# Value matmuls of four attention heads together, in two column parts, inside a transformer kernel on one core

## The reference, cut to what matters

```
scores = jnp.einsum('bhqd,bhkd->bhqk', q, k) * hs ** (-0.5)
p = jax.nn.softplus(scores)
p = p * p
causal = jnp.tril(jnp.ones((t, t), dtype=p.dtype))
p = p * causal
attn = p / (jnp.sum(p, axis=-1, keepdims=True) + 1e-09)
out = jnp.einsum('bhqk,bhkd->bhqd', attn, v)
```

## Time and profile before

| | us |
|---|---|
| median of three runs | 1726.71 |
| the profiled execution, its own time | 1729.62 |
| span of its profile | 1727.8 |
| attention phase, first score matmul to last divide | about 275.6 to 748.9 |

### The profile page before, as it was taken

The page is one execution under the profiler, slowest core; times in us unless marked ns, Lnnn a source line. Parts: engine busy times, 40 slices in busy tenths (PEclk is TensorE's granted clock), DMA queues, the critical chain, the costliest instruction groups (busy, mean ns, idle before and its releaser), DMA issues. The chain is left out here.

```text
span 1727.8 us, 28806 instructions
## 1 busy us (share of the span) xinstructions
PE 1643.6 (95%) x11141; PEld 1148.6 (66%) x11188; DVE 1244.1 (72%) x2350; ACT 878.2 (51%) x1356; POOL 412.0 (24%) x382
## 2 busy tenths in 40 slices
PE   8999888999999999999999999998999999899998
PEld 7888775333333433378887777776777777677786
DVE  4545897677777777656556888876877777788886
ACT  3332687666666666643232322218888887622210
POOL 0002112121212111140004422211455555311111
PEclk9999999999999999999999999999999999999999
DMA  5000266646363554200001000001322333200000
GB/s 158 14 1 13 74 195 133 88 52 96 50 90 59 79 69 73 27 1 13 1 1 41 27 1 1 1 1 64 99 99 99 99 100 115 82 13 13 25 25 25
DMA packets 57160, 95.82 MB, mean 55 GB/s; under 512 B 7904, under 2 KB 29632, under 8 KB 57024
## 3 DMA queue, kind: packets, MB, share of 16 engines
q1 hardware_dynamic: 56064, 93.38, 24.4%
q10 hardware_dynamic: 960, 0.59, 0.1%
HBM read 76.91 MB, written 17.04 MB: 54 GB/s over the span
## 5 line engine op out<-in xcount | busy, mean ns | idle before, releaser
L1405 ACT ACTIVATE att_weights<-ps 128x1024 f32<-128x1024 f32 (+1 forms) x288 | 280.7, 976 | 157.1 <-PE ps L1346 83.0
L1432 DVE TENSOR_TENSOR att_weights<-att_weights 128x1024 f32<-128x1024 f32 (+1 forms) x240 | 298.5, 1262 | 67.8 <-ACT att_weights L1405 67.1
L1366 PE MATMUL ps<-att_weights,att_v_ones 64*32 64x64 f32 (+5 forms) x2048 | 286.8, 398 | 6.2 <-DVE v L1453 6.2
L928 DVE SCALAR_TENSOR_TENSOR X<-ps,moe_gsel,X 128x256 f32<-128x256 f32 x512 | 246.1, 483 | 63.5 <-PE ps L48 40.4
L48 PE MATMUL ps<-w_experts_hi,moe_xh 128*128 128x512 f32 x512 | 204.9, 400 | 0.6 <-DVE X L928 0.6
L48 PE MATMUL ps<-w_experts_hi,moe_xl 128*128 128x512 f32 x512 | 203.1, 397 | 0.0
L48 PE MATMUL ps<-w_experts_lo,moe_xh 128*128 128x512 f32 x512 | 201.4, 393 | 0.0
L1366 PEld LDWEIGHTS ps<-att_weights,att_v_ones 128*32 128x32 f32 (+1 forms) x2048 | 81.8, 108 | 124.7 <-issue 74.1
L424 ACT ACTIVATE ffn_gates<-ps,ffn_gate_bias 128x512 f32<-128x512 f32 x72 | 49.5, 688 | 148.3 <-PE ps L48 126.6
L1495 POOL TENSOR_TENSOR att_weights<-att_weights 128x1024 f32<-128x1024 f32 x16 | 30.3, 1892 | 378.0 <-ACT att_weights L1405 378.0
L48 PEld LDWEIGHTS ps<-w_experts_hi,moe_xh 128*128 128x128 f32 x512 | 96.1, 188 | 27.4 <-DVE X L928 4.0
(11 more groups left out here) (281 smaller groups left out, 3726.8 us busy)
## 6 DMA issues: line engine op xcount, KB each, us to landing
ssm_lb<-decays SPq DMA_DIRECT2D x32, 512.0 KB, 4.6
ssm_rise<-decays SPq DMA_DIRECT2D x28, 512.0 KB, 3.9
qk_parts<-qkv_part SPq DMA_DIRECT2D x32, 384.0 KB, 2.8
q_stack<-qk_parts SPq DMA_DIRECT2D x64, 128.0 KB, 4.6
k_stack<-qk_parts SPq DMA_DIRECT2D x64, 128.0 KB, 7.9
att_q_stack<-qk_parts SPq DMA_DIRECT2D x64, 128.0 KB, 4.6
att_k_stack<-qk_parts SPq DMA_DIRECT2D x64, 128.0 KB, 8.4
out<-X SPq DMA_DIRECT2D x7, 512.0 KB, 3.2
```

What stands on the lines that cost most here:

```text
L928: dve.scalar_tensor_tensor(out=x, in0=ring[:, e // 2, (e % 2) * C:(e % 2 + 1) * C], scalar=gsel[:, s, j, e:e + 1], in1=x, op0=ALU.mult, op ...
L1366: ins = pe.matmul(O(qb)[h * 2 * HD:(h + 1) * 2 * HD, q0:q0 + w], values, Wt[rows, u % WU, t, c:c + w], start=kj == 0 and part == FULL, sto ...
L1405: act.activation(Wt[:, u % WU, 0:n], scores(u)[:, 0:n], ACT.Softplus).then_inc(p_done, 1)
L1432: dve.tensor_tensor(wt, wt, wt, ALU.mult).then_inc(sq_done["dve"], 1)
```

## The change

The values of a step's four heads are now computed together, in the order of the steps and not of the units. A step's matmuls are cut into two parts by columns, and one part is issued behind each of the two score units that are issued with the step: a FULL step into columns 0 to 255 and 256 to 511 of all four heads, a REST step into its first and second key tile. The FULL step of the first key tile, whose matmuls start the sums, is not cut: all of it is the second part. UPPER steps have one part, as before. A step's part 0 waits for the squares of both its units.

Scores run four steps ahead (`STEPS_AHEAD`), in place of seven units. The turn of a block comes two units behind its end in place of four. ScalarE squares units 6, 9 and 14 in place of 8 and 14; VectorE has 14 of a pass's 18 units in place of 15.

```diff
-    AHEAD = 7
-    TURN_LAG, COPY_LAG, DEN_LAG, OUT_LAG = 4, 7, 9, 10
+    step_units = [[u for u in range(NU) if step_of[u] == m] for m in range(NS)]
+    STEPS_AHEAD = 4
+    TURN_LAG, COPY_LAG, DEN_LAG, OUT_LAG = 2, 7, 9, 10
...
-    BY_ACT, BY_POOL = (8, 14), (11,)
+    BY_ACT, BY_POOL = (6, 9, 14), (11,)
...
-            def value_unit(i, u):
-                m = step_of[u]
+            def value_part(i, m, part_no, parts):
                 s, (qb, last, products) = m // PS, pass_steps[m % PS]
+                upper = products[0][-1] == UPPER
+                if part_no == 0:
+                    value_waits(i, m, s, qb, products, upper)
+                if products[0][-1] == FULL and parts == 2 and products[0][1] == 0:
+                    products = products if part_no else []
+                elif products[0][-1] == FULL and parts == 2:
+                    at = part_no * (BANK // 2)
+                    products = [(h, kj, unit, t, c + at, q + at, BANK // 2, part) for h, kj, unit, t, c, q, w, part in products]
+                elif parts == 2:
+                    at = part_no * len(products) // 2
+                    products = products[at:at + len(products) // 2]
+                for h, kj, unit, t, c, q, w, part in products:
+                    q0 = q - qb * BANK
...
+                    ins = pe.matmul(O(qb)[h * 2 * HD:(h + 1) * 2 * HD, q0:q0 + w], values,
+                                    Wt[rows, (s * PU + unit) % WU, t, c:c + w], start=kj == 0 and part == FULL, stop=part == UPPER and kj == (qb + 1) * GT - 1)
+                if part_no == parts - 1:
+                    ins.then_inc(pv_done, 1)
+
+            def value_waits(i, m, s, qb, products, upper):
+                if m % PS == 0:
                     pe.wait_ge(v_copied, 2 * (2 * i + s + 1))
-                if products[0][1:3] == (0, u % PU) and products[0][-1] != UPPER:
+                if products[0][1] == 0 and not upper:
                     pe.wait_ge(o_done, (i * 2 + s) * BLOCKS + qb + 1)
                     if qb == 0:
                         pe.matmul(O(qb), ident16[:, :], neg[:, 0:1].broadcast_to([P, BANK]), start=True, stop=False)
-                pe.wait_ge(sq_done[squarer[u]], squares(squarer[u], i, u))
-                if products[0][-1] == UPPER:
+                for u in step_units[m]:
+                    pe.wait_ge(sq_done[squarer[u]], squares(squarer[u], i, u))
+                if upper:
                     pe.sem_inc(squared, 1)
...
             def body(i, first=False, last=False):
-                for u in range(NU):
-                    if not (last and u + AHEAD >= NU):
-                        score_unit(i, u + AHEAD)
-                    value_unit(i, u)
-                    outputs_at(u, BLOCK_UNITS, NU, TURN_LAG, i, first, turn_output)
+                for m in range(NS):
+                    ahead = m + STEPS_AHEAD
+                    coming = [] if last and ahead >= NS else step_units[ahead % NS]
+                    parts = len(step_units[m])
+                    for n in range(2):
+                        if n < len(coming):
+                            score_unit(i + ahead // NS, coming[n])
+                        if n < parts:
+                            value_part(i, m, n, parts)
+                    for u in step_units[m]:
+                        outputs_at(u, BLOCK_UNITS, NU, TURN_LAG, i, first, turn_output)
...
-            for u in range(AHEAD):
-                score_unit(0, u)
+            for m in range(STEPS_AHEAD):
+                for u in step_units[m]:
+                    score_unit(0, u)
```

More of the change, by code:

```diff
@@ L1347, in score_unit @@
                 ins.then_inc(s_done, 1)
-            def value_unit(i, u):
-                m = step_of[u]
+            def value_part(i, m, part_no, parts):
                 s, (qb, last, products) = m // PS, pass_steps[m % PS]
-                if u % PU == 0:
+                upper = products[0][-1] == UPPER
[11 more added lines that the diff above has]
+                    q0 = q - qb * BANK
+                    rows = slice(h % 2 * HALF, (h % 2 + 1) * HALF) if part == UPPER else slice(0, P)
+                    values = va_up[rows, s, kj, h // 2] if part == UPPER and h % 2 else va[rows, s, kj, h]
+                    ins = pe.matmul(O(qb)[h * 2 * HD:(h + 1) * 2 * HD, q0:q0 + w], values,
[4 more added lines that the diff above has]
+                if m % PS == 0:
                     pe.wait_ge(v_copied, 2 * (2 * i + s + 1))
-                if products[0][1:3] == (0, u % PU) and products[0][-1] != UPPER:
+                if products[0][1] == 0 and not upper:
                     pe.wait_ge(o_done, (i * 2 + s) * BLOCKS + qb + 1)
```

## The result

The changed kernel takes **1615.35 us** (median of 4 runs, 1613.91 to 1618.04) against 1726.64 for the kernel before beside it: ratio 0.9354, 95% interval 0.9335 to 0.9373. 1613 was forecast. The profiled execution took 1616.52 us.

What follows compares the result with a forecast made beforehand. TensorE was taken to set each pass: 29.57 us becomes 21.58 plus 0.63 waiting for ScalarE, 22.2. Over 16 passes, with less saved in the last, 1726.7 - 114 = 1613 us, range 1602 to 1641.

Steps and rivals of the forecast that it cites:

- Full speed for four: TensorE's value matmuls: four heads side by side take 0.45 us a part, so eight steps fall from 14.24 to 7.20.
- rival B: Value matmuls: four wide is not full speed while other engines work; at 0.8, a pass of 24.0, 1641 us; chance 0.07.
- Rival C: Value matmuls: heads still start in pairs whatever their order; a pass of 28.6, 1711 us; chance 0.02.
- Switches and the output wait: TensorE: 0.10 us gaps between scores and values fall from 3.60 to 3.00 a pass; the 0.41 wait for divided output goes.
- ScalarE's stretch: Softpluses and squares from softplus 6 to 11 run without idle time; TensorE waits 0.6 us before unit 14's scores.
- The turn's cover: At the earlier turn, VectorE's copy is there at 2.0 and TensorE arrives at 2.4: covered by 0.4 us only.
- rival A: Hand-overs between engines: late turn 0.5 us, output wait stays, ScalarE's stretch costs double; a pass of 24.2, 1644 us; chance 0.21.
- VectorE: Its work in a pass falls from 21.2 to 20.1 us with one square less, under the 22.2 of the pass.
- rival D: TensorE's clock falls in new waits: slower, 1897 us with all of the phase at the low level; chance 0.03.
- Loads. Covered.: A pass's 2.1 MB of q and k stacks load in 15 to 17 us; the shorter pass leaves 22.
- The likeliest case: The forecast's own case for the attention passes: from no wait, 21.58 a pass (1602), to 22.8 (1621); chance 0.67.

Runs made afterwards that it cites:

- pairs: The changed kernel with a step's two parts again two pairs of heads over all columns, in place of four heads together: 1686.23 us (one run).
- one-block kernel: The changed kernel with a step's values in one block behind its second score unit: 1608.08 us; also with ScalarE squaring 8, 14 and an earlier copy: 1600.85 us.
- (8, 14): The changed kernel with ScalarE squaring units 8 and 14 in place of 6, 9 and 14: 1622.64 us, ratio 0.9394.
- paced: Each stack load piece waits for more score units: changed kernel 1613.41 us; one-block kernel with ScalarE squaring 8, 14 and an earlier copy 1593.4 us.

## Why the prediction was right

**Full speed for four (rival B).** Right: a part of 256 columns 0.57 with its switch against 0.55 of the sum, and at pairs the pass is 4.66 longer. By rival B's 0.8 the pass would have been 24.0; it is 22.29. Rival C's 28.6 fell by the same rows.

**Switches and the output wait.** Right: 0.10 at each switch that was read, and no wait for the divide in the list of waits. The one-block kernel bears the price out: with 10 blocks in place of 15 it has ten switches fewer, 1.0 us at 0.10. Its pass is 0.81 shorter although the reported wait for ScalarE is 0.41 longer, which makes 1.2; the other 0.2 I can't assign.

**ScalarE's stretch.** Right to 0.07 us at each of its eight steps: with the start of unit 7's scores at 484.28 as time 0, softplus 8 was forecast at 487.27 and starts at 487.25, softplus 11 at 490.98 and starts at 490.91. TensorE's wait is 0.60 against 0.63. The other squares of the experiments move that wait, to 0.25 with (8, 14).

**The turn's cover.** Right, 0.46 against 0.4, but the text didn't say what it hangs on. One square ahead of the copy uses it up, 0.67 a pass; that is rival A's late turn, one wait of its three, and it came only where unit 6's square went back to VectorE.

**VectorE.** 19.4 us in 22 makes 19.7 a pass against 20.1; 21.2 in 22 still don't set the pass. The clock (rival D) stayed at 1.00 from 305 us on.

**What the sum missed.** A pass is 22.29 and not 22.21, and the first one 22.77, where the wait before unit 14's scores is reported as 1.22 us, not 0.43. "Loads. Covered." asked only whether the loads end in time; they do, but TensorE stood twice amid them, as inferred above for its instructions, and that cost 3.2 us. Together the phase saved 109.2 us in place of 114.7. The whole came nearer, 111.3 by the medians, and that is partly luck: in the profiled executions 3.9 us of the difference came from outside the phase, where nothing was changed. The likeliest case's range, 1602 to 1621, held the time.

## What to carry to other kernels

When a stage has one engine at its limit, add up that engine's matmuls and gaps until the sum meets the measured period; a change is then priced by its terms. Walk the next engine through the stage unit by unit, since its average (here 18.6 us in 22.2) hides the stretch where it is late. Where a wait sits on a small instruction in an in-order queue, look at what stands ahead of it there before moving work to another engine: the copy one place earlier gave more than a third square on ScalarE.

## What the runs showed that I had not expected

TensorE can stand 0.6 to 2.7 us with no semaphore to blame while loads for a later pass are queued on the DMA engines. It did so in every unpaced kernel with four heads together that loads its stacks; the kernel before and the one with pairs issue the same loads at once too, in longer passes (29.57 and 26.95), and have none: no wait over 0.41 between 300 and 725 us, and none at all between 300 and 680. The same bytes in the same time kept the DMA engines busy for 0.71 (the changed kernel) and 0.69 (one block) of 300 to 600 us when the 16 pieces were issued at once, and for 0.51 and 0.58 when paced. Pacing removed all such waits and cost nothing that the runs show: the undisturbed pass is 22.29 and 20.89 with it as without.
